# The sum of two experts' results on one core: its chunk loop written out with doubled buffers, and its transposed rows left in on-chip memory for the next stage

## What is computed

```python
x = layernorm(x + attention_0(x))       # three attentions, blended
x = layernorm(x + moe_0(x))             # 8 experts, top 2 per token
x = layernorm(x + memory_attention(x))  # chunks of 64, a memory per head
x = layernorm(x + moe_1(x))             # 16 experts, each takes its best tokens
```

```python
q, k, v = (heads(x @ W.T) for W in (Wq, Wk, Wv))
k = k / maximum(norm(k), 1e-12)
```

## Time and profile before

| | us |
|---|---|
| median of the runs | 4403.63 |
| profiled execution, its own time | 4404.2 |
| its span, first to last instruction | 4402.5 |
| PE busy | 3749.4 |
| DVE busy | 2359.5 |
| ACT busy | 1472.2 |
| POOL busy | 1507.8 |

### The profile page before, as it was taken

How to read it: one execution, slowest core, us unless ns; L and a number is a source line. 1 busy time by engine, 2 the same in 40 slices (tenths; PEclk the granted TensorE clock), 3 DMA queues, 4 the chain that set the end, 5 groups by cost and what they waited for, 6 DMA issues and landing times. The chain is left out here.

```text
span 4402.5 us, 56081 instructions
## 1 busy us (share of the span) xinstructions
PE 3749.4 (85%) x18715; PEld 1758.6 (40%) x18715; DVE 2359.5 (54%) x3949; ACT 1472.2 (33%) x2141; POOL 1507.8 (34%) x1303
## 2 busy tenths in 40 slices
PE   8989999989999789996679455577897998999994
PEld 3412222213332333333445255333455565565552
DVE  5579999955554145552442548756794671111113
ACT  2247777763333223332223224111452311111111
POOL 0032222235666126664246213032661322222221
PEclk9979999999999999998789666788897999999997
DMA  4543222311110521102422621333452104333323
GB/s 168 194 74 67 68 68 66 70 22 62 39 39 13 189 96 39 40 26 80 133 69 84 206 97 40 129 89 88 138 165 102 43 30 137 83 108 93 99 81 86
DMA packets 316311, 387.35 MB, mean 88 GB/s; under 512 B 56208, under 2 KB 244896, under 8 KB 314592
## 3 DMA queue, kind: packets, MB, share of 16 engines
q1 hardware_dynamic: 260800, 292.64, 21.3%
q0 software_dynamic: 35232, 69.77, 6.4%
q10 hardware_dynamic: 20096, 22.55, 1.5%
HBM read 240.68 MB, written 135.76 MB: 86 GB/s over the span
## 5 line engine op out<-in xcount | busy, mean ns | idle before, releaser
L571 DVE TENSOR_REDUCE modulated_mx<-modulated_ring 128x1 f32<-128x512 f32 x1024 | 651.9, 683 | 52.0 <-PE modulated_ring L478 46.3
L555 ACT ACTIVATE modulated_probs<-modulated_scores 128x1024 f32<-128x1024 f32 x512 | 496.1, 1021 | 181.9 <-PE modulated_scores L499 181.9
L2961 DVE TENSOR_TENSOR expert_h<-expert_gelu,expert_bank 128x512 f32<-128x512 f32 x128 | 88.1, 688 | 390.3 <-PE expert_bank L2929 387.5
L508 PE MATMUL modulated_acc<-modulated_probs,modulated_v 128*32 128x512 f32 x2048 | 273.5, 606 | 0.6 <-ACT modulated_probs L555 0.6
L499 PE MATMUL modulated_scores<-modulated_q,modulated_k 128*128 128x512 bf16 x1024 | 268.3, 384 | 1.0 <-DMA modulated_q<-modulated_turned 0.4
L478 PE MATMUL modulated_ring<-modulated_k,modulated_q 64*128 64x512 bf16 x1024 | 239.5, 399 | 34.6 <-DMA modulated_v<-scratch_v 23.3
L2889 POOL DMA_INDIRECT scratch_acc<-expert_y,expert_idx x64 | 100.9, 1577 | 483.1 <-DVE expert_y L2966 441.0
L910 POOL TENSOR_TENSOR meta_total<-meta_total,meta_probs 128x1024 f32<-128x1024 f32 x96 | 225.7, 2351 | 86.5 <-ACT meta_probs L831 85.5
L910 POOL TENSOR_TENSOR causal_total<-causal_total,causal_probs 128x1024 f32<-128x1024 f32 x96 | 225.6, 2350 | 86.5 <-ACT causal_probs L831 85.5
L2929 PE MATMUL expert_bank<-expert_xT,expert_wg 128*128 128x512 f32 x512 | 243.2, 597 | 7.8 <-ACT expert_xT L2941 7.8
L853 DVE TENSOR_REDUCE meta_mx<-meta_maxima 128x2 f32<-128x1024 f32 x120 | 146.0, 1217 | 185.3 <-PE meta_maxima L737 185.3
(11 more groups left out here) (471 smaller groups left out, 6815.8 us busy)
## 6 DMA issues: line engine op xcount, KB each, us to landing
expert_wg<-x_WgT SPq DMA_DIRECT2D x16, 1024.0 KB, 4.9
expert_wu<-x_WuT SPq DMA_DIRECT2D x16, 1024.0 KB, 7.0
expert_wd<-x_WdT SPq DMA_DIRECT2D x16, 1024.0 KB, 5.2
modulated_k<-scratch_k_part SPq DMA_DIRECT2D x192, 64.0 KB, 3.0
modulated_q<-scratch_q_part SPq DMA_DIRECT2D x192, 64.0 KB, 3.1
scratch_v<-proj_v SPq DMA_DIRECT2D x8, 1024.0 KB, 6.6
modulated_v<-scratch_v SPq DMA_DIRECT2D x16, 512.0 KB, 4.9
scratch_M<-steps_snap SPq DMA_DIRECT2D x16, 512.0 KB, 3.2
```

The lines of the kernel that those rows point to most:

```text
L508: last = nc.tensor.matmul(acc[32 * j:32 * j + 32, :], vs[g % SLOTS][:, t, j, :], probs[u % NPROBS][j // 2][:, j % 2, :], start=(t == 0), s ...
L555: nc.scalar.activation(probs[u % NPROBS][i][:], sc[i][:], ACT.Exp, scale=SCALE).then_inc(s_exp, 1)
L571: V.tensor_reduce(mx[h % 2][:, x // 2, 1 - j % 2, j // 2, x % 2:x % 2 + 1], ring[bank_of["max", 4 * m + j]][:], AX.X, ALU.max).then_inc(s_ ...
```

## The change

The loop of `add_routed` is written out over the 8 chunks, with constants in all waits (`Order` in place of `Steps`). `part`, `y`, `new` and the statistics now exist twice as well. On DVE the sum and the statistics of chunk k + 1 stand ahead of the reciprocal and the normalizing of chunk k. The store of x2 moves from ACT's queue to SP's, where it stands behind the loads of chunk k + 2 and ahead of those of chunk k + 3; the order of a chunk's three loads is now ya, x, yb. ACT copies the transposed rows from PSUM into two tiles of SBUF (`x2_turned0` and `1`, 16 KB per partition each) that stay allocated over both stages. The stores to x2T, their tensor, the four loads of it in `memory_projections` and the wait for them are gone.

The core of the diff (moved helper class and unchanged parts left out):

```diff
 def add_routed(nc, io, scr):
...
-        x, ya, yb = ([st.sb(f"{n}{j}", [P, TT, D]) for j in range(2)] for n in ("x", "ya", "yb"))
-        part, y = st.sb("part", [P, TT, D]), st.sb("y", [P, TT, D])
-        new, newT = st.sb("new", [P, TT, D]), st.sb("newT", [P, KD, CH])
+        x, ya, yb, part, y, new = (two(n, [P, TT, D]) for n in ("x", "ya", "yb", "part", "y", "new"))
...
+        sums = lambda k: by_token("first", k) + by_token("summed", k) + by_token("stats", k) + by_token("aggr", k) + [("eps", k)] if k < NCH else []
+        dve_names = sums(0)
+        for k in CHUNKS:
+            dve_names += sums(k + 1) + [("inverse", k)] + by_token("normed", k)
...
         @block.sync
         def _(sp):
+            def load(k):
+                if k >= 2:
+                    dve_s.wait(sp, ("summed", k - 2, TT - 1))
+                for to, from_ in ((ya, scr["y2"][0:N]), (x, scr["x1"]), (yb, scr["y2"][N:2 * N])):
+                    sp.dma_start(to[k % 2][:], tokens(from_, k)).then_inc(s_loaded[k % 2], 16)
+
             load_all(sp, [(shares[:], scr["shares"])], s_in)
-            for s in loaded:
-                s.start(sp)
-            with sp.Fori(0, NCH // 2) as i:
-                for j in range(2):
-                    dve_s.wait(sp, i, (j, "summed", TT - 1), back=1)
-                    loaded[j].done(sp.dma_start(x[j][:], by_token(scr["x1"], i, j)))
-                    loaded[j].done(sp.dma_start(ya[j][:], by_token(scr["y2"][0:N], i, j)))
-                    loaded[j].done(sp.dma_start(yb[j][:], by_token(scr["y2"][N:2 * N], i, j)))
+            load(0)
+            load(1)
+            for k in CHUNKS:
+                if k + 2 < NCH:
+                    load(k + 2)
+                dve_s.wait(sp, ("normed", k, TT - 1))
+                sp.dma_start(tokens(scr["x2"], k), new[k % 2][:]).then_inc(s_st[k % 2], 16)
+            for j in range(2):
+                sp.wait_ge(s_st[j], 16 * (NCH // 2))
...
         @block.scalar
         def _(act):
-            act_s.start(act)
-            stored.start(act)
-            storedT.start(act)
-            with act.Fori(0, NCH // 2) as i:
-                for j in range(2):
-                    dve_s.wait(act, i, (j, "eps"))
-                    act_s.done(nc.scalar.activation(std[:], var[:], ACT.Sqrt), (j, "sqrt"))
-                    dve_s.wait(act, i, (j, "normed", TT - 1))
-                    stored.done(act.dma_start(by_token(scr["x2"], i, j), new[:]))
-                    storedT.wait(act, 2 * i + j, back=1)
-                    for m in range(KD):
-                        mm.wait(act, i, (j, "turn", m))
-                        act_s.done(nc.scalar.activation(newT[:, m, :], bank[j][m][:], ACT.Copy), (j, "turn", m))
-                    act_s.wait(act, i, (j, "turn", KD - 1))
-                    storedT.done(act.dma_start(rows(scr["x2T"])[:, :, bass.ts(2 * i + j, CH)], newT[:]))
-            stored.wait(act, NCH - 1)
-            storedT.wait(act, NCH - 1)
+            for k in CHUNKS:
+                dve_s.wait(act, ("eps", k))
+                act_s.done(nc.scalar.activation(std[k % 2][:], var[k % 2][:], ACT.Sqrt), ("sqrt", k))
+                at = k * CH % GROUP
+                for m in range(KD):
+                    mm.wait(act, ("turn", k, m))
+                    act_s.done(nc.scalar.activation(scr["xT"][k * CH // GROUP][:, m, at:at + CH], bank[k % 2][m][:], ACT.Copy), ("turn", k, m))
...
+            sum_and_measure(0)
+            for k in CHUNKS:
+                if k + 1 < NCH:
+                    sum_and_measure(k + 1)
+                j = k % 2
+                act_s.wait(dve, ("sqrt", k))
+                dve_s.done(V.reciprocal(inv[j][:], std[j][:]), ("inverse", k))
+                dve_s.wait(dve, ("inverse", k))
+                if k >= 2:
+                    dve.wait_ge(s_st[j], 16 * (k // 2))
+                    mm.wait(dve, ("turn", k - 2, KD - 1))
+                for t in range(TT):
+                    dve_s.done(V.tensor_scalar(new[j][:, t, :], y[j][:, t, :], mv[j][:, t, 0:1], inv[j][:, t:t + 1], ALU.subtract, ALU.mult), ("normed", k, t))
...
 def memory_projections(nc, io, scr):
...
-        xT = two("xT", [P, KD, GROUP])
+        xT = scr["xT"]
...
-            for kd in range(KD):
-                sp.dma_start(xT[0][:, kd, :], scr["x2T"][kd * P:(kd + 1) * P, 0:GROUP]).then_inc(s_x[0], 16)
             load_all(sp, weights[2:], s_wide)
-            for kd in range(KD):
-                sp.dma_start(xT[1][:, kd, :], scr["x2T"][kd * P:(kd + 1) * P, GROUP:2 * GROUP]).then_inc(s_x[1], 16)
...
-                if kind == "k" and c == 0:
-                    pe.wait_ge(s_x[g], 16 * KD)
```

More of the change, by code:

```diff
@@ L102, in done, with __init__, wait @@
         return dma.then_inc(self.sem, 16)
+class Order:
+    def __init__(self, sem, names, passed):
+        self.sem, self.passed, self.at = sem, passed, 0
+        self.value = {x: n + 1 for n, x in enumerate(names)}
+        assert len(self.value) == len(names)
+    def done(self, ins, name):
+        self.at += 1
+        assert self.value[name] == self.at, (name, self.at)
+        return ins.then_inc(self.sem, 1)
+    def wait(self, eng, name, alone=False):
+        eng.wait_ge(self.sem, self.value[name])
+        if alone:
+            apart(eng, self.passed)
 class Stage:
@@ new lines, in add_routed @@
+        by_token = lambda name, k: [(name, k, t) for t in range(TT)]
+        turns = [("turn", k, m) for k in CHUNKS for m in range(KD)]
+        sums = lambda k: by_token("first", k) + by_token("summed", k) + by_token("stats", k) + by_token("aggr", k) + [("eps", k)] if k < NCH else []
+        dve_names = sums(0)
+        for k in CHUNKS:
+            dve_names += sums(k + 1) + [("inverse", k)] + by_token("normed", k)
+        order = lambda n, names: Order(st.sem(n), names, scr["passed"])
+        mm, dve_s = order("mm", turns), order("dve", dve_names)
@@ L1590, in _ @@
             pe.wait_ge(s_made, 2)
[L1591 to L1596, removed]
+            for k in CHUNKS:
+                dve_s.wait(pe, ("normed", k, TT - 1))
+                for m in range(KD):
+                    if k >= 2:
+                        act_s.wait(pe, ("turn", k - 2, m))
@@ L1623, in _, with sum_and_measure @@
             V = nc.vector
[L1624 to L1638 removed]
+            def sum_and_measure(k):
+                j = k % 2
+                dve.wait_ge(s_loaded[j], 48 * (k // 2 + 1))
+                share = lambda c, t: shares[:, c, k * TT + t:k * TT + t + 1]
+                for t in range(TT):
+                    dve_s.done(V.scalar_tensor_tensor(part[j][:, t, :], ya[j][:, t, :], share(0, t), x[j][:, t, :], ALU.mult, ALU.add), ("first", k, t))
+                for t in range(TT):
+                    dve_s.wait(dve, ("first", k, t))
+                    dve_s.done(V.scalar_tensor_tensor(y[j][:, t, :], yb[j][:, t, :], share(1, t), part[j][:, t, :], ALU.mult, ALU.add), ("summed", k, t))
+                for t in range(TT):
+                    dve_s.wait(dve, ("summed", k, t))
+                    dve_s.done(V.bn_stats(stats[j][:, t, :], y[j][:, t, :]), ("stats", k, t))
+                for t in range(TT):
+                    dve_s.wait(dve, ("stats", k, t), alone=True)
+                    dve_s.done(V.bn_aggr(mv[j][:, t, :], stats[j][:, t, :]), ("aggr", k, t))
+                dve_s.wait(dve, ("aggr", k, TT - 1))
+                dve_s.done(V.tensor_scalar(var[j][:], mv[j][:, :, 1], EPS, None, ALU.add), ("eps", k))
@@ L3044, in build @@
     routed_experts(nc, io, scr)
-    add_routed(nc, io, scr)
-    memory_projections(nc, io, scr)
+    with ExitStack() as held:
+        scr["xT"] = [held.enter_context(nc.sbuf_tensor(f"x2_turned{g}", [P, KD, GROUP], F32)) for g in range(N // GROUP)]
+        add_routed(nc, io, scr)
+        memory_projections(nc, io, scr)
     memory_steps(nc, io, scr)
```

57 lines of the change are left out of this document (15 added, 42 removed).

## The result

| | before | changed |
|---|---|---|
| median of 20 runs each | 4405.90 us | 4397.82 us |
| lowest and highest | 4402.14 to 4408.20 | 4390.74 to 4402.76 |
| ratio, 95% interval | | 0.9982, 0.9975 to 0.9989 |
| span of the profiled execution | 4402.5 us | 4396.3 us |

The change gains 8.1 us by the medians, by the interval 5 to 11 us. The forecast was 10.9 us and 4392.7 us, with a range to 4397.0; the measured median lies 0.8 above that range. The kernel before itself came out 2.3 us above the median of 3 runs from which I reckoned (4405.90 against 4403.63).

The account below looks back on a forecast made before the run. It took the path of loads, DVE chain with store waits, copy, x2T store and reload, k projection as the bound. Terms 1.4 + 0.7 + 2.6 + 6.2 = 10.9 us gave 4392.7 us, range 4387.0 to 4397.0.

Parts of the forecast that it names:

- (a): Stage start: without loop entry and semaphore starts, the first load and DVE begin 1.4 us earlier.
- (b): DVE chain: reordered, square root hidden behind the next sum, 6.66 us per chunk instead of 6.88, eight chunks 53.4 us.
- (c): SP's loads behind the x2 store: late at chunks 3, 5 and 7, three stalls of 1.75 us, 5.3 in all.
- (d): Stage end: last tile to next stage 3.4 us instead of 6.05, the x2 store now last; gain 2.6 us.
- (e): Projections' start: PE waits for the alphas, 2.9 us after the stage's first transfer instead of 9.17; gain 6.2 us.
- my bounds of 7.4 and 8.6: SP's queue, store plus three loads: 7.4 us if the store hides completely, 8.6 for four transfers back to back.
- The rival that half of it would be lost there: Projections: only part of the stage starts early, half of 6.2 us is lost, about 4396 to 4399; chance 0.06.
- No load stall: Rival for the chunk chain: load sets land within 6.66 us; gain 16.2 us, time 4387.4; chance 0.18.
- Fetch of code: Rival: one or two uncovered code fetches on DVE or SP, 2.5 to 5 us, 4395.2 to 4397.7; chance 0.12.
- Slower: Rival: store and loads on SP's queue take 12 us, three stalls cost 16 us and cancel all gains; chance 0.02.

Follow-up runs that it names:

- loads ahead of the store: Changed kernel with SP issuing the loads of chunk k + 3 before waiting for chunk k to be normalized and storing it; 4389.15 us, ratio 0.9966 against before.
- the written-out order alone: Changed kernel with the x2T store (on ACT's queue, two buffers) and its reload put back; 4408.03 us, ratio 1.0014 against before.
- the best order: Changed kernel with next chunk's square root ahead of ACT's copies and loads ahead of SP's store; 4388.33 us, ratio 0.9965 against before, stage 62.90 us.
- Idle work: Both order edits plus unread transposes after chunks and 6 unread matmuls before the projections: 4382.19 us, ratio 0.9952; without transposes between the last two chunks 4383.58, 0.9958.

## Why the prediction was right or wrong

The working against the profile of the changed kernel:

| step | forecast us | measured us |
|---|---|---|
| (a) earlier start of DVE after the shares | 1.4 | 9.31 - 7.20 = 2.1 |
| (b) eight chunks without waits | 53.4 | 52.5 |
| (c) three load waits | 5.3 | 6.1 |
| (b) square root hidden | 0 | 2.8 at the last chunk |
| (d) last tile to next stage | 3.4 | 2538.48 - 2535.20 = 3.3 |
| (e) stage start to first k matmul | 3.0 | 2.85 |
| gain up to the first k matmul | 10.9 | 83.97 - 74.77 = 9.2 |

The step that failed is in (b): the wait for the square root, put at nothing for all eight chunks, is 2.78 us at the last. Together (b) and (c) were to give back 0.7 us; the chain from DVE's first sum to the last tile took 61.44 us instead of 59.44 and cost 2.0.

**(a)** was right in cause. The first load left 1.5 us sooner after the shares (0.39 us instead of 1.88). The other 0.6 us I had not forecast: the last load of the first set was issued another 0.1 us sooner and landed 0.5 us sooner after its issue.

**(b) failed in one place.** The square root "being hidden behind the next sum" holds for seven chunks and not for the eighth. I had counted ACT's work per chunk as lying beside DVE's and had not followed ACT's order through the last round, where the sum that covers it is missing. That is 2.8 us, the largest error of the sum, the same in all three profiles of the changed kernel, and taking the root first removed it. A chunk without a wait took 6.50 us against my 6.66. Its instructions are no faster: the sum reaches the epsilon after 4.92 us (2478.78 to 2483.70), before after 4.93. I had let the next instruction wait for the end of the one that adds the epsilon, 0.17 + 0.05 us; one that needs nothing of it begins 0.08 us after its start (2483.78).

**(c) was right**, in cause, place and nearly in size: waits at 3, 5, 7 and none at 2, 4, 6, in two of the three profiles. From the moment at which DVE could go on (2485.28) to its start with chunk 3 (2493.73) are 8.45 us; I had said 8.4. The transfers behind the first such store (512 KB each, us to landing):

```profile
scratch_x<-blend_new SPq DMA_DIRECT2D x1, 512.0 KB, 3.5
blend_ya<-scratch_y SPq DMA_DIRECT2D x1, 512.0 KB, 5.2
blend_x<-scratch_x SPq DMA_DIRECT2D x1, 512.0 KB, 6.0
blend_yb<-scratch_y SPq DMA_DIRECT2D x1, 512.0 KB, 6.5
```

The last one was issued 1.81 us behind the store, so from store to last landing are 8.3 us, between my bounds of 7.4 and 8.6. The rule of the Trainium skill (DMA: Bandwidth & Descriptors, Queues, rings and completion order) that one ring is served in order fits with this. What I had made of it, a store served wholly ahead and 2.4 us for each of the three waits, came out only at chunk 5 (2.48 us), and at 3 and 7 they were 1.86 and 1.80. That the store ahead of the loads is what costs was shown by the order of issue, not by the rule. In the second profile of the changed kernel the three waits are 1.66, 2.01 and 1.64 us; in the third they make 4.7 us in all, and part of it had moved to chunks 4 and 6 (0.25 and 0.84 us).

**(d) and (e)** were right within 0.15 us. The start of the k projections moved up by 10.3 us on average (84.0, 84.0 and 85.6 us after the shares before; 74.8, 74.4 and 73.6 changed), and the first store of kT by 10.3 us too, so nothing of it was lost. The projections as a whole took 283.3 instead of 289.9 us on average, 6.5 less. The rival that half of it would be lost there falls.

**The rivals.** No load stall: did not happen, but is what loads ahead of the store give. Fetch of code: no gap on DVE without a releaser; the instructions of a written-out chunk take as long as in the loop. Slower: the changed kernel is not; the written-out order alone is, by 0.14%, with 10.2 us of load waits and 3.3 us for the root, where my rival had waits of 16 us.

**The number.** The absolute time was missed by 5.1 us: 2.3 because the median of 3 runs of before was low, and 2.8 in the gain. Either of them alone would have kept the time inside the range: with the right base the range would have ended at 4399.3, and with the square root hidden the time would be 4395.0 by an estimate that lets its 2.8 us go through to the end. The base was a mistake of mine: 20 runs of the kernel before spread over 6 us and of the changed one over 12, and its median moves by up to 5 us between rounds. I had taken nothing for that into the range; 3 runs within 2 us had looked like a still kernel.

That the two stages gained 10.4 us against my 10.9 is partly luck. In the first profile the square root (2.8) and the load waits (0.8) took 3.6 us from the sum, and the start (0.7), the shorter chunk (0.9) and the two ends (0.3) gave 1.9 back, which leaves 9.2 at the first k matmul. The rest came from executions that differ: in the third profile of before the store waits are 6.6 us instead of 5.1, and in the third of the changed kernel the load waits are 4.7 instead of 6.1. The interval of the ratio, 4.8 to 11.0 us, includes 10.9 at its edge.

The spread lies in the projections (3 to 4 us between profiles of one kernel), the chunk attention (7) and the stages ahead of the change (4 before, 2 changed, by the time of the first load of the shares). It goes with the granted clock, as the 24 timed runs of before show; what makes the clock differ stays open. Which part of the difference between 10.4 us in the profiles and 8.1 in the medians is chance is open as well.

## What to carry to other kernels

When the work of the next chunk is put ahead of the rest of this one, follow each engine's order through the last round too: the work that hid a late result is missing there. A store on the same queue as the next loads belongs behind them if the loads could go earlier; its wait holds back everything that stands after it. A round trip through main memory between two stages costs at both ends, landing of the store and of the load. Removing it brought the first k matmul 12.0 us forward with the loop unchanged; the best order on top of that took another 6.1 us off the stage. And a time that differs between two single profiles is an effect only where more profiles of the unaltered kernel don't show the same difference.

## What the hardware showed that I had not expected

Idle work did bring the clock up, and bought nothing up to the end of the k matmuls it was meant for: 32 matmuls ran in 7.5 instead of 9.2 us, and the first store of kT, which needs their results, left at the same moment, 105.7 us after the shares. The same 12 records of idle matmuls took 2.83 us where PE had run idle and real transposes almost without a pause up to 1.0 us before them, and 4.65 us where it had stood still for 2.8 us ahead of the last sixteen transposes.

The projections take two lengths in executions of one and the same kernel, 3 us apart, in a stretch of 85 or 88 us whose instructions no edit changed.

Removing the x2T stores alone, with the loop unchanged, cut the waits for another store from 5.1 to 1.2 us. At a DMA share of 0.90 in the loop, the x2 stores of chunks 1 and 3 landed 7.0 and 6.4 us after their issue, and with the x2T stores gone (share 0.76) both landed after 5.0; that of chunk 4 did not gain (5.5 and 5.8). So a transfer that nobody waits for delayed ones that are waited for. Both stores leave on ACT's queue; whether the queue or the DMA engines behind it are where they met was not tested.
